# Two heads on the two array halves, one projection per pair, and a rope whose swap of neighbours is done by DMA

## The reference, cut to what matters

```python
q = jnp.einsum('bse,fe->bsf', x, w_q).reshape(B, S, H, E)
k = jnp.einsum('bse,fe->bsf', x, w_k).reshape(B, S, H, E)
v = jnp.einsum('bse,fe->bsf', x, w_v).reshape(B, S, H, E)
q, k = _apply_rope(q, cos, sin), _apply_rope(k, cos, sin)
att = jnp.einsum('bqhd,bkhd->bhqk', q, k) / jnp.sqrt(jnp.asarray(E, x.dtype))
att = jax.nn.softmax(jnp.where(causal, att, -jnp.inf), axis=-1)
y = jnp.einsum('bhqk,bkhd->bqhd', att, v).reshape(B, S, H * E)
return jnp.einsum('bsf,ef->bse', y, w_o)
# _apply_rope, on neighbours (a, b) of the features: (a*c - b*s, a*s + b*c)
```

## Time and profile before

| what | value |
|---|---|
| time of the runs | 3906.31, 3925.68 and 3928.64 us, median 3925.68 |
| profiled execution | span 3932.8 us from its first to its last instruction, 7.1 above the median of the runs; no other time is listed for it |
| busy share of the span | PE 86%, PEld 60%, DVE 63%, POOL 43%, ACT 37% |
| mean granted clock of PE | 0.92 of 2.4 GHz |
| HBM | read 258.31 MB, written 23.27 MB |

### The profile page before, as it was taken

How to read it: one execution, slowest core, us unless ns; L and a number is a source line. 1 busy time by engine, 2 the same in 40 slices (tenths; PEclk the granted TensorE clock), 3 DMA queues, 4 the chain that set the end, 5 groups by cost and what they waited for, 6 DMA issues and landing times. The chain is left out here.

```text
span 3932.8 us, 69093 instructions
## 1 busy us (share of the span) xinstructions
PE 3385.7 (86%) x21387; PEld 2365.0 (60%) x21387; DVE 2484.0 (63%) x4247; ACT 1442.3 (37%) x2188; POOL 1702.7 (43%) x1424
## 2 busy tenths in 40 slices
PE   6336999999999999999999999999999569999998
PEld 1124555555555555555555555555555359898887
DVE  2346666676666767666766766667676556464646
ACT  0002333333333333333333333333333235454545
POOL 0464555555555555555555555555555320000000
PEclk8557999999999999999999999999999779999999
DMA  2524454445545544444554445455555624333333
GB/s 78 165 85 138 120 133 127 131 125 129 137 119 133 135 126 128 130 132 118 138 134 124 126 129 136 120 132 135 125 130 124 136 70 135 101 133 102 119 123 103
DMA packets 289629, 487.77 MB, mean 124 GB/s; under 512 B 95336, under 2 KB 113144, under 8 KB 289304
## 3 DMA queue, kind: packets, MB, share of 16 engines
q1 hardware_dynamic: 257160, 398.26, 36.8%
q0 software_dynamic: 32400, 88.52, 9.4%
HBM read 258.31 MB, written 23.27 MB: 72 GB/s over the span
## 5 line engine op out<-in xcount | busy, mean ns | idle before, releaser
L1108 ACT ACTIVATE attention_probs<-attention_pss 128x896 f32<-128x896 f32 (+4 forms) x768 | 623.0, 811 | 1320.9 <-PE attention_pss L957 1310.4
L1165 DVE TENSOR_REDUCE attention_mx<-attention_pss 128x2 f32<-128x1024 f32 (+3 forms) x520 | 525.5, 1022 | 377.8 <-PE attention_pss L970 208.1
L1041 PE MATMUL attention_psY<-attention_probs,attention_xt 128*64 128x128 f32 (+7 forms) x4386 | 733.5, 440 | 2.1 <-DMA attention_xt<-xt 1.8
L1283 POOL DMA_INDIRECT attention_gat<-table,attention_idx x585 | 559.8, 957 | 191.6 <-issue 118.8
L954 PE MATMUL attention_pss<-attention_QA,attention_KA 128*128 128x512 f32 (+4 forms) x1536 | 554.1, 416 | 49.5 <-ACT attention_probs L1108 43.7
L1696 DVE SCALAR_TENSOR_TENSOR spectral_eo<-spectral_psE,spectral_sig,spectral_eo 64x512 fp32r<-64x512 f32 x512 | 383.9, 750 | 263.8 <-ACT spectral_eo L1675 259.2
L1264 POOL TENSOR_TENSOR attention_nat_l<-attention_qk,attention_nat_h 128x512 fp32r<-128x512 f32 x260 | 425.3, 1636 | 259.3 <-ACT attention_nat_h L1127 259.3
L970 PE MATMUL attention_pss<-attention_nat_h 64*128 64x512 f32 (+2 forms) x1560 | 350.7, 451 | 201.7 <-DVE attention_mx L1165 198.2
L1599 PE MATMUL spectral_psE<-spectral_tz,spectral_up 128*128 128x256 f32 (+2 forms) x3072 | 507.5, 324 | 4.3 <-DVE spectral_eo L1696 4.3
L1256 POOL TENSOR_TENSOR attention_qk<-attention_tA,attention_tB 128x512 f32<-128x512 f32 x260 | 411.1, 1592 | 203.5 <-DVE attention_tB L1180 201.9
L1599 PEld LDWEIGHTS spectral_psE<-spectral_tz,spectral_up 128*128 128x128 f32 x3072 | 470.7, 188 | 44.9 <-DVE spectral_eo L1696 6.1
(11 more groups left out here) (194 smaller groups left out, 3862.4 us busy)
## 6 DMA issues: line engine op xcount, KB each, us to landing
attention_QA<-attention_nat_h SPq DMA_DIRECT2D x520, 128.0 KB
spectral_tz<-phis SPq DMA_DIRECT2D x128, 320.5 KB, 4.7
spectral_tz<-phis SPq DMA_DIRECT2D x128, 320.0 KB, 4.3
attention_xb<-xn SPq DMA_DIRECT2D x66, 512.0 KB, 4.0
attention_wt<-wsplit SPq DMA_DIRECT2D x66, 512.0 KB, 5.9
attention_KA<-attention_nat_h SPq DMA_DIRECT2D x260, 128.0 KB
attention_KB<-attention_nat_h SPq DMA_DIRECT2D x260, 128.0 KB
attention_KA<-attention_nat_l SPq DMA_DIRECT2D x260, 128.0 KB
```

The lines of the kernel that those rows point to most:

```text
L1041: ins = pe.matmul(psY[C * half:C * half + C, c0:c1], xt[:, kt_, :], probs[:, q + c0:q + c1], start=first, stop=(j == NS - 1), skip_group_c ...
L1108: act.activation(probs[:, pstep[j]:pstep[j] + width], pss[:, slot, lead:lead + width], ACT.Exp, scale=float(E) ** -0.5).then_inc(s_act, 1)
L1165: ins = dve.tensor_reduce(mx_far[:, :, i - 4] if k0 else mx[:, :, i], scores, AX.X, ALU.max)
L1283: pool.indirect_dma_start(gat[:, n, :, :].rearrange("p q c -> p (q c)"), None, d.table.rearrange("r q c -> r (q c)"), bass.IndirectOffsetO ...
```

## The change

- Steps are worked through for both heads of a pair in turn: S of head 0, S of head 1, then the next step. `probs` holds three steps of two heads.
- The value product no longer cuts the queries: head 0 uses one half of the array and head 1 the other, so that `psY` and `yT` hold two heads, and one copy on ACT (`leave`) evacuates both.
- `wo` becomes block-diagonal for a pair: one matmul per token tile projects both heads (130 columns instead of 65), in two units `out` 0 (six tiles) and `out` 1 (two tiles).
- The rope is projected once: no swapped weights. A unit `rope` c holds keys and queries of one half of the tokens. DVE multiplies by sine into tB and by cosine into tA; SP's `swap` r copies tB with odd and even partitions exchanged into `qk`, two DMAs per r; POOL's `add` then adds tA to `qk` in place. swap r waits for lower r - 2, which reads the same half of `qk`.
- All units stand in a new order, `UNITS`, one list for each of the 12 half steps, and so do uppers, the convolution's operations and POOL's gathers.

The core of the diff:

```diff
-DEFORM_AT = {(0, 0): ["m0", "m1"], (0, 1): ["m2"], (0, 2): ["a"], (1, 0): ["s"]}
-POOL_ORDER = [("add", 0), ("add", 1), ("lower", 0), ("add", 2), ("lower", 1), ("gather", 0), ("add", 3), ("lower", 2), ("lower", 3), ("token", 0), ("gather", 1), ("token", 1), ("gather", 2)]
-UPPER_AT = {1: [0, 1], 3: [2], 5: [3]}
+UNITS = [
+    [("rope", 0)],
+    [("rope", 1)],
+    [("out", 0)],
+    [("out", 1)],
+    [("max", "b")],
+    [("max", "ac"), ("max", "d")],
+    [("max", "e"), ("dT",)],
+    [("max", "f"), ("max", "g"), ("dR",)],
+    [("max", "h"), ("max", "i")],
+    [("max", "j"), ("max", "k")],
+    [("row",)],
+    [("dX",)],
+]
+DEFORM_AT = {2: ["m0"], 3: ["m1", "m2"], 4: ["a0"], 5: ["a1"], 9: ["s"]}
+POOL_ORDER = [("add", 0), ("add", 1), ("lower", 0), ("add", 2), ("lower", 1), ("gather", 0), ("add", 3), ("lower", 2),
+              ("lower", 3), ("token", 0), ("token", 1), ("gather", 1), ("gather", 2)]
+UPPER_AT = {3: [0, 1], 4: [2, 3]}
+PV_AT = {2 * j + 3: j for j in range(NS - 1)}
+LAST_PV = 1
...
+                def swap(r, done, first=False):
+
+                    if not first or r > 1:
+                        wait_apart(sp, s_low, done + (r - 1), s_apart)
+                    wait_apart(sp, s_turn, done + (r + 1), s_apart)
+                    for odd in range(2):
+                        sp.dma_start(qk[odd:P:2, r % 2, :], tB[1 - odd:P:2, r % 2, :]).then_inc(s_swap[r % 2], 16)
...
                             pp = 1 - k
+                            for r in range(4):
+                                swap(r, 8 * it + 4 * (1 + k))
                             wait_apart(sp, s_full, it * N_BODY + (N_AHEAD + summed[k]), s_apart)
...
-                        for a in range(2):
+                        for i in range(2):
+                            w = ROPE_OF[2 * c + i][0]
                             for part in range(2):
-                                ins = pe.matmul(out[:, a * HB:(a + 1) * HB], wt[:, pp, part, 2 * (1 - w) + a, :],
+                                ins = pe.matmul(out[:, i * HB:(i + 1) * HB], wt[:, pp, part, 1 - w, :],
                                                 xb[:, pp, c * HB:(c + 1) * HB], start=(part == 0), stop=(part == 1))
...
-                    for t in range(NT):
-                        ins = pe.matmul(out[:, t * P:t * P + E + 1], yT[:, buffer, t * P:(t + 1) * P], wo[:, head, :],
+                    for n, t in enumerate(range(6) if part == 0 else range(6, NT)):
+                        at = HB * (n // 3) + 2 * OUT * (n % 3)
+                        ins = pe.matmul(out[:, at:at + 2 * OUT], yT[:, buffer, t * P:(t + 1) * P], wo[:, pair, :],
                                         start=True, stop=True)
...
-                    for n, (half, kt_, c0, c1) in enumerate(halves(j)):
...
+                    for kt_, at, c0, c1 in values(j):
+                        for h in range(2):
+                            ins = pe.matmul(psY[C * h:C * h + C, c0:c1], xt[:, kt_, :], probs[:, h, at + c0:at + c1],
+                                            start=(j == 0), stop=(j == NS - 1), skip_group_check=True)
...
+                        for i in range(2):
+                            r = 2 * u[1] + i
...
+                            dve.wait_ge(s_sum, R + r + 1)
+                            dve.tensor_tensor(tB[:, r % 2, :], pss[:, slot, i * HB:(i + 1) * HB], sinT[:, cols],
+                                              ALU.mult).then_inc(s_turn, 1)
+                            dve.tensor_tensor(tA[:, r % 2, :], pss[:, slot, i * HB:(i + 1) * HB], cosT[:, cols],
+                                              ALU.mult).then_inc(s_dve if i else s_cos, 1)
...
-                    if not isinstance(pair, int) or 4 * pair + r > 1:
-                        wait_apart(pool, s_low, 4 * pair + (r - 1), s_apart)
-                    pool.wait_ge(s_dve, read)
-                    pool.tensor_tensor(qk[:, r % 2, :], tA[:, r % 2, :], tB[:, r % 2, :], ALU.add).then_inc(s_sum, 1)
+                    pool.wait_ge(s_swap[r % 2], 64 * pair + 32 * (r // 2 + 1))
+                    if r % 2:
+                        wait_apart(pool, s_dve, read, s_apart)
+                    else:
+                        wait_apart(pool, s_cos, 2 * pair + (r // 2 + 1), s_apart)
+                    pool.tensor_tensor(qk[:, r % 2, :], qk[:, r % 2, :], tA[:, r % 2, :], ALU.add).then_inc(s_sum, 1)
```

More of the change, by code:

```diff
@@ L597, with step_units @@
 DEF_STEPS = NORMED + 2
-PV_LAG = 2
 KQ_COPIES = 16 * (2 * 6 + 2 * 4)
[L602 to L607, removed]
+def step_units(n):
+    return [("S", n % 2, n // 2)] + UNITS[n]
+ORDER = [(k, n, u) for k in range(BODY_PAIRS) for n in range(NB) for u in step_units(n)]
+AHEAD = [(1, NB - 1, ("rope", r)) for r in range(2)] + [(1, NB - 1, u) for u in PAIR_MAX + [("row",)]]
 N_BODY, N_AHEAD = len(ORDER), len(AHEAD)
@@ L666, in widths @@
 def widths(step):
     return sum(S - P * j for j in STEPS[step])
[L670 to L673, removed]
-def exp_read(head, step):
-    at = ORDER.index((head % BODY_HEADS, step, ("S", step)))
-    return reads_before(ORDER, at + 1, True) - (ACT_BODY if head < 0 else 0)
-def place(head, unit):
-    return [(h, u) for h, _, u in ORDER].index((head, unit))
+assert all(widths(j) <= (PROBS_AT + (PROBS,))[j % 3 + 1] - PROBS_AT[j % 3] for j in range(NS))
@@ new lines, in values, with of_last, exp_read @@
+def values(step):
+    first = PROBS_AT[step % 3]
+    out = []
+    for t in STEPS[step]:
+        out += [(t, first - P * t, c0, c1) for c0, c1 in by_bank(P * t, S)]
+        first += S - P * t
+    return out
+def of_last(places):
+    return max(j for j, tiles in enumerate(STEPS) if any(t in places for t in tiles))
+XT_LAST = (of_last(range(4)), of_last(range(4, NT)))
+XT_FIRST = tuple(min(j for j, tiles in enumerate(STEPS) if any(t // 4 == half for t in tiles)) for half in range(2))
+def exp_read(k, step):
+    at = ORDER.index((k % BODY_PAIRS, 2 * step + 1, ("S", 1, step)))
+    return reads_before(ORDER, at + 1, True) - (ACT_BODY if k < 0 else 0)
@@ L801, in _ @@
                 act.wait_ge(s_wvo, 1)
-                act.activation(wo[:, :, 0:E], pss[:, 0, :].rearrange("p (h e) -> p h e", h=HEADS), ACT.Copy).then_inc(s_wvo, 1)
+                for n in range(2):
+                    rows = slice(C * n, C * n + C)
+                    act.activation(wo[rows, :, OUT * n:OUT * n + E],
+                                   pss[rows, 0, :].rearrange("p (g n e) -> p g n e", n=2, e=E)[:, :, n, :],
+                                   ACT.Copy).then_inc(s_wvo, 1)
             @block.gpsimd
@@ L933, in _, with unit @@
                     sp.wait_ge(s_xt[half], 16 * B + 16)
+                    sp.wait_ge(s_swap[half], 64 * (2 * NIT + 1))
             @block.tensor
             def _(pe):
-                def unit(h, u, slot, it, head=None):
+                def unit(k, u, slot, it, pair=None):
                     kind = u[0]
                     out = pss[:, slot, :]
-                    k = h // 2
                     pp = 1 - k
                     if kind == "S":
-                        j = u[1]
-                        if j == 0 and h % 2 == 0:
+                        _, h, j = u
+                        if j == 0 and h == 0:
                             pe.wait_ge(s_dup, KQ_COPIES * (2 * it + k) + KQ_COPIES)
@@ L1099, in unit, with leave @@
-                def unit(h, u, slot, n, it):
+                def leave(it, k):
+                    act.wait_ge(s_pv, 2 * NS * it + (NS * k + NS))
+                    act.activation(yT[:, 1 - k, :], psY[:, :], ACT.Copy).then_inc(s_y, 1)
+                def unit(k, u, slot, n, it):
                     if u[0] == "S":
-                        j = u[1]
+                        _, h, j = u
                         width = widths(j)
@@ L1159, in unit @@
+                def unit(k, u, slot, n, R, seen, before=None):
                     if u[0] not in BY_ACT:
```

327 lines of the change are left out of this document (146 added, 181 removed).

## The result

The changed kernel takes 4469.83 us (median of 4 runs, 4468.86 to 4473.28) beside 3916.21 us of the kernel before on the same chip: ratio 1.141, 95% interval 1.137 to 1.144. The forecast was 4410 in a range of 4150 to 4700. The profiled execution has a span of 4468.8 us, 536.0 more than the one before.

What follows compares the result with a forecast made beforehand. A chain through four engines was to stall PE 11.7 us per pair; with PE work, short waits, cold clock and 1.0, 50.6 us per pair, 7.5 more: 480 + 5 on 3932.8 is 4418, less 7 for the median: 4410 us, range 4150 to 4700.

Steps and rivals of the forecast that it cites:

- The mechanism: Attention pair: upper 3 waits for add 3 behind gathers and a1, delaying the exponential that frees PE's slot; case chance 0.84.
- The stall: PE before scores (0,3), whose slot exp (1,2) must read: idle 11.7 us in every pair, t = 17.2 to 28.9.
- Its chain: Upper 0, lower 0, swap 2, add 2, lower 1, a1, gather 0, add 3, upper 3: ends at t = 27.8.
- The early half: Rope 0, swaps 0 and 1, their adds and rope 1's products: done at 9.4, before PE wants the slot at 10.6, so free.
- The clock: PE resuming after the stall is granted half clock at first: 2.5 us more in each of 64 pairs.
- What PE saves: PE's work per pair: rope -2.1, output -1.2, values -1.0, sum -4.3 us (-2.1 to -5.9), from 37.5 to 33.2.
- The rival in which the chain doesn't bind: Attention stage: PE works through, upper 3 ending by t = 17; 38.2 us per pair, 3610 us in all; chance 0.10.
- The sum: Attention pair: stall, PE work, end waits, cold clock and 1.0 added give 50.6 us, 7.5 more than before.
- a flat 1.0: Added to each pair for activation table loads every second pair and slower matmuls after short waits: 1.0 us.
- The 5 us ahead of the first pair: Before the first attention pair the chain runs once more with two swaps in series, 2 x 2.35 = 5 us.
- lower end: Low bound of the chain case: a1 at 20, no cold clock, end waits covered; 46.5 us per pair, 4145 us.

Runs made afterwards that it cites:

- The experiment: Changed kernel with 34 unused matmuls of 512 columns put on PE ahead of the scores that stall: 4282.47 us, ratio 1.094.
- the version with all three moves: Changed kernel with uppers 2 and 3 moved later, SP's swaps laid between the copies, and gather 0 moved behind add 3 and lower 2: 3826.38 us, 0.978.
- both edits together: Changed kernel with uppers 2 and 3 moved later and SP's swaps laid between the copies: 3832.5 us, ratio 0.979.
- The version of 3790 us: All three moves (uppers, swaps between copies, gathers), plus the value product of step 2 one half step earlier: 3790.3 us, ratio 0.967.

## Why the prediction was right

Times t count from a pair's first scores (1018.94).

- **The mechanism** is the one forecast, link by link. The moves of UPPER_AT, of the gathers and of the DMAs, one at a time, show which of its links bind: ACT's place decides, the gathers carry 3.0 us, and, each in the changed kernel's order, swaps 0.4 and copies nothing. What I had wrong in the picture is that ACT's idle time is in two pieces, 5.07 us before the third upper and 7.24 before the fourth, where I had looked for about 10 before the fourth alone. And of the two links that end at the gathers, a1 and lower 1, a1 binds by 0.88 us only (1.0 on average).
- **The stall**: forecast 11.7 us from 17.2 to 28.9; measured 11.54, from 17.8 to 29.3.
- **Its chain**: lower 0 ended at 15.6 instead of 14.3, because upper 0 ended at 13.5 instead of 12.8 and lower 0 then took 2.05 us beside DVE's m1 and m2. Add 2 began 3.07 us behind it where I had 2.35 for a swap. a0 took 1.34 us instead of 2.3, since it ran in POOL's wait for that swap, and a1 1.24 instead of 0.76, beside lower 1. These nearly cancel, which is luck and not forecast: a1 ended at 21.8 (forecast 21.2), add 3 began at 26.5 (25.8), upper 3 ended at 28.5 (27.8).
- **The early half**, called free, was: rope 1's products ended at 11.0 instead of 9.4. The first sine ended 1.1 us late, as the pair's first matmuls still ran at half clock, and add 0 began 3.05 us behind it where I had 2.35 for the swap; no one on PE waited for them there.
- **The clock**: 2.5 us per resumption forecast; from 1048.27 to the next pair 22.3 us passed, 3.7 of them idle (0.32, 1.22, 1.50 and 0.63), which leaves 18.7 for work that I had put at 16.1 at full clock: 2.6. The experiment gave 2.9. The clock stayed at 1.00 longer into the idle time than the 2 us that I had read from the earlier trace rows: PE is idle from 1036.73 on, and the mean is still 0.66 within 1040 to 1041. Nothing in the sum hung on it. The Trainium skill (TensorE: Matmul & The Clock Gate, HAM oscillation) describes a loop in which each burst of matmuls starts at half clock behind its wait. The stage's mean clock of 0.83 agrees.
- **What PE saves**: forecast -4.3 us per pair. Its busy share times the pair's length was 0.912 x 43.1 = 39.3 us before and is 0.846 x 41.4 = 35.1 (2200.6 of 2600 us busy) in the version with all three moves: -4.2, at a clock of 0.93 there against 0.95 before. By part: four rope matmuls take 1.01 us at full clock (1025.40 to 1026.41), so eight fewer are -2.0 (forecast -2.1). Twelve projections take 1.48 us (1027.08 to 1028.56), 0.12 each, hardly more than the 0.113 of half the columns: with 0.41 for the other four -1.7 (forecast -1.2). What is left for the values, as a remainder and not measured by itself, is -0.5 (forecast -1.0). The rival in which the chain doesn't bind had this saving right, and needed the order mended in two places.
- **The sum**: 51.7 us per pair instead of 50.6. The difference is 0.4 by the stall's later end, 0.1 by the clock, and 0.6 by waits of 3.7 us behind it where I had 2.1 and a flat 1.0. The 5 us ahead of the first pair didn't come; that part is 1.5 us shorter, and the part behind the last pair 9.7.
- **The range**: its lower end was added up wrongly. With a1 at 20, no cold clock and the last waits covered, the same terms give 20 + 7.7 + 16.1 + 1.0 = 44.8 us per pair and not 46.5, so about 4035 us and not 4145. The measurement lies far from that end.

## What to carry to other kernels

When several engines work through fixed lists, cost a move by asking what stands behind the moved step on its own engine: an operation that waits for a long chain (upper 3) must not stand before one that frees a resource of the busiest engine (the exponential). After one wait is removed, read the waits again before giving a size: the next one in line, here SP's copies, may take back more than half (264 us came of 637), and only both edits together turned 14% slower into 2% faster. A stall of the matrix engine costs more than its length, here a quarter more, since the work behind it runs at half clock.

## What the runs showed of the hardware beside this

The clock also falls behind short waits, and late. Windows of the changed kernel over the end of a pair:
```profile
1068.20:1069.70 1.50, 0.01 (x1) 0.02 (x1) 1.19 (x7) 0.92 (x1) 0.00 (x0) 1.00 0.01 3
...
1070.60:1072.00 1.40, 1.39 (x4) 0.87 (x4) 0.02 (x1) 0.00 (x0) 0.00 (x0) 0.66 0.26 68
1072.00:1074.00 2.00, 2.00 (x6) 1.24 (x5) 0.00 (x0) 1.42 (x2) 0.00 (x0) 0.50 0.01 1
1074.00:1076.00 2.00, 2.00 (x10) 0.61 (x9) 1.57 (x3) 0.89 (x1) 0.00 (x0) 0.89 0.00 0
```

PE has idle times of 1.22, 1.50 and 0.63 us there, and its clock is still 1.00 in them; it falls after PE has resumed, to 0.50 in 1072 to 1074, and the scores then take 0.87 and 1.06 us where they take 0.72 and 0.76 one pair earlier. The long stall is not needed for this: with the unused matmuls in its place, PE has the same waits of 1.50 and 0.63 us before a pair, and 0.50 from 1030 to 1032 behind them. The version of 3790 us still has it: the first scores of the pair looked at take 1.22 and 1.05 us.

The releaser that the trace names needs a second look where a wait has two candidates: of 38 waits of ACT for an upper's input in 1000 us it puts 25 down to POOL's add (133.9 us) and 13 to a copy from `nat_h` to QA (94.6 us). In the timeline the last upper starts 1.3 us after add 3, its duration.

DVE and POOL hold each other up. The step a0 took 1.34 us while POOL waited, and 2.31 in the earlier trace rows; m1 and m2 took 2.89 us together beside a lower, which itself took 2.05 instead of 1.26. The Trainium skill (SBUF — State Buffer, Who interferes with whom) has a DVE operation with two SBUF inputs contend with a POOL operation that reads SBUF. These rows agree nearly with one waiting for the other: one after the other they would be 2 x 0.95 (m0 alone) + 1.26 = 3.2 us, and it was 2.9 from the first start to the last end.

An issue of a 64-partition copy between SBUF tiles takes SP 0.6 us, so the 8 of the swaps and the 24 copies are about 20 us of each pair on one queue.
